# A two-layer transformer kernel: six of the first attention's maxima earlier, constant rows on ACT, one block for keys and heads, earlier first products and a finer last store

## The reference

```python
x = L0_attn_x                                   # 2 x 1024 x 512
xn = _layernorm(x)
x = x + attn0(xn) + ffn0(xn)                    # 16 heads of 32, 4 key heads, full softmax;
                                                # silu(xn@W1.T) * (xn@W3.T), Hadamard, @W2.T
xn = _layernorm(x)
x = x + attn1(xn) + ffn1(xn)                    # 16 heads of 128 (two halves of 64), window 128,
                                                # relu(a1 - lam*a2) renormalised;
                                                # shared expert + top 4 of 32 experts
```

## Time and profile before

| what | value |
|---|---|
| median of 3 runs | 2629.05 us (2627.87 to 2630.51) |
| profiled execution, its own time | 2627.59 us |
| its span | 2625.8 us |
| PE busy | 2483.7 us (95%) |
| DVE, ACT, POOL busy | 1737.8, 1100.6, 1037.9 us |

### The profile page before, as it was taken

One profiled execution on the slowest core, in us unless ns is written; L12 is line 12 of the kernel. 1 busy time (PEld: TensorE's weight loads), 2 busy tenths in 40 slices (PEclk: granted clock), 3 DMA queues, 4 the chain that ended last, 5 costly groups with the idle time before them and its releaser, 6 DMA issues. The chain is left out here.

```text
span 2625.8 us, 35942 instructions
## 1 busy us (share of the span) xinstructions
PE 2483.7 (95%) x12212; PEld 1702.1 (65%) x12212; DVE 1737.8 (66%) x3817; ACT 1100.6 (42%) x2815; POOL 1037.9 (40%) x827
## 2 busy tenths in 40 slices
PE   6899999999799999998989999889999799999998
PEld 3444444444488888886767777667777556657886
DVE  6677676765355555556459999759999633336886
ACT  1246464645233333332327777627777511111111
POOL 2359787876311111110027676525454300002442
PEclk9989999999899999999999999999999999999999
DMA  5722222213200000001212100010000198873111
GB/s 182 243 51 41 57 41 41 41 21 128 105 17 16 16 16 16 16 1 53 74 56 72 35 29 13 18 53 12 17 17 1 39 327 301 295 254 94 49 25 64
DMA packets 170343, 193.64 MB, mean 74 GB/s; under 512 B 85582, under 2 KB 115278, under 8 KB 169792
## 3 DMA queue, kind: packets, MB, share of 16 engines
q1 hardware_dynamic: 158656, 178.90, 22.0%
q0 software_dynamic: 11520, 12.64, 1.5%
HBM read 161.95 MB, written 54.53 MB: 82 GB/s over the span
## 5 line engine op out<-in xcount | busy, mean ns | idle before, releaser
L653 DVE TENSOR_REDUCE neg<-bank 128x1 fp32r<-128x1024 f32 x256 | 300.9, 1214 | 120.7 <-PE bank L556 120.7
L703 ACT ACTIVATE probs<-bank 128x512 f32<-128x512 f32 x512 | 277.8, 595 | 243.9 <-PE bank L566 242.0
L494 POOL TENSOR_TENSOR probs<-probs 128x1024 f32<-128x1024 f32 x128 | 302.8, 2388 | 136.1 <-PE bank L575 135.6
L1643 POOL TENSOR_SCALAR mix<-mix,sm 128x256 f32<-128x256 f32 (+1 forms) x256 | 233.0, 922 | 174.7 <-DVE sm L1541 174.2
L1584 ACT ACTIVATE ms<-ms,sm 128x256 f32<-128x256 f32 (+1 forms) x512 | 247.6, 486 | 111.8 <-DVE sm L1512 110.9
L881 POOL TENSOR_TENSOR up_lo<-up_raw,up_hi 128x1024 fp32r<-128x1024 f32 x16 | 46.2, 2905 | 392.6 <-ACT up_hi L869 392.6
L566 PE MATMUL bank<-q_parts,k_parts 97*128 97x512 f32 x512 | 187.4, 445 | 0.7 <-ACT probs L703 0.7
L1512 DVE CUSTOM_DVE_ANT_0 ms<-bank,misc 128x256 f32<-128x256 f32 (+1 forms) x512 | 184.7, 399 | 2.3
L566 PEld LDWEIGHTS bank<-q_parts,k_parts 97*128 97x128 f32 x512 | 86.9, 189 | 146.2 <-ACT probs L703 84.4
L556 PE MATMUL bank<-k_parts,q_parts 96*128 96x512 f32 x512 | 152.8, 419 | 7.8 <-DVE neg L653 5.9
L1883 POOL TENSOR_TENSOR up_lo<-up_raw,up_hi 128x1024 fp32r<-128x1024 f32 x11 | 26.2, 2381 | 334.5 <-ACT up_hi L1852 334.5
(11 more groups left out here) (227 smaller groups left out, 5841.6 us busy)
## 6 DMA issues: line engine op xcount, KB each, us to landing
ewg<-in_L_ffn_Wg_dram SPq DMA_DIRECT2D x32, 704.0 KB, 6.8
ewu<-in_L_ffn_Wu_dram SPq DMA_DIRECT2D x32, 704.0 KB, 8.0
ewd<-in_L_ffn_Wd_dram SPq DMA_DIRECT2D x32, 512.0 KB, 5.1
q_parts<-qk_dram SPq DMA_DIRECT2D x48, 256.0 KB, 4.4
w_dram<-w_parts SPq DMA_DIRECT2D x16, 512.0 KB, 3.5
up_raw<-in_L_ffn_W_dram SPq DMA_DIRECT2D x16, 512.0 KB, 4.1
ewd<-in_L_ffn_Wd_dram SPq DMA_DIRECT2D x32, 192.0 KB, 5.3
qk_dram<-qk_hi SPq DMA_DIRECT2D x20, 256.0 KB, 2.3
```

The costliest lines, as they stand in the source:

```text
L494: pool.tensor_tensor(probs[:, even, half, :], probs[:, even, half, :], probs[:, odd, half, :], ALU.add).then_inc(S["paired"], 1)
L653: dve.tensor_reduce(neg[:, U % HPT, q:q + 1], bank[:, 2 * (n % 2):2 * (n % 2) + 2, :], AX.XY, ALU.max, negate=True).then_inc(S["max"], 1)
L703: act.activation(probs[:, s % BUFS, j, :], bank[:, 4 + j % 2, :], ACT.Exp, scale=scale).then_inc(S["exps"], 1)
L1643: pool.tensor_scalar(mix[:, p % 2, h, 0:w], mix[:, p % 2, h, 0:w], sm[:, p % 3, 8 + h:9 + h], None, ALU.mult).then_inc(S["probs"], 1)
```

## The change

- The tile `neg` is allocated in the outer scope. In the last chunk of the projection PE makes `early_peaks(f)` behind each of its six products, in banks 4 and 5, and DVE `early_maximum(f)` behind each rotation and, for the last, behind the copy of the values. `heads0` then begins with n = 6 (`EARLY0`).
- POOL no longer fills the rows of ones; ACT writes them, as copies of a broadcast one, in chunk 1 behind the high parts of tiles 3 and 4.
- In both feed-forwards PE waits for a new tile's high part, and for its low part only ahead of the products that read it.
- In the second attention the two blocks of each half become one. PE waits for the rotated keys ahead of the first scores, and in the second half for the reloaded values ahead of the first weighing; SP no longer waits for them.
- In the last step of the second feed-forward PE signals each of the four tiles, DVE waits for each, and SP stores the last chunk tile by tile.

```diff
+EARLY0 = 6
...
+        t["neg"] = sb(ctx, "neg", [P, HPT, CH // P], F32R)
...
+            def early_peaks(n):
+                u, q = n // SUBS, n % SUBS
+                if n == 0:
+                    wait(pe, env["h0"]["q_loaded0"], 48)
+                    wait(pe, env["h0"]["k_loaded0"], 48)
+                wait(pe, env["h0"]["max"], n)
+                for h in range(2):
+                    mm = pe.matmul(bank[:, 4 + h, :], t["qp"][0:3 * HD0, u, q * P:(q + 1) * P],
+                                   t["kp"][0][0:3 * HD0, u % KV0, h * CH:(h + 1) * CH], start=True, stop=True)
+                mm.then_inc(env["h0"]["peaks"], 1)
...
+                    if c == NC - 1:
+                        early_peaks(f)
...
+            def early_maximum(n):
+                wait(dve, env["h0"]["peaks"], n + 1)
+                dve.tensor_reduce(t["neg"][:, n // SUBS, n % SUBS:n % SUBS + 1], bank[:, 4:6, :], AX.XY, ALU.max,
+                                  negate=True).then_inc(env["h0"]["max"], 1)
...
                     turn(c, f)
+                    if not more:
+                        early_maximum(f)
...
                 dve.tensor_copy(vT[:, :], bank[:, NR % 4, :]).then_inc(S["read"], 1)
+            early_maximum(NR)
...
                     act.activation(hi[:, n % KEPT, :], rot[:, f % 2, :], ACT.Copy).then_inc(S["hi"], 1)
+                    if c == 1 and f >= NR - BATCH:
+                        row = t["kp"][f - (NR - BATCH)][3 * HD0:3 * HD0 + 1, :, :].rearrange("p j s -> p (j s)")
+                        act.activation(row, env["ones"][3 * HD0:3 * HD0 + 1, 0:1].to_broadcast([1, KV0 * SEQ]),
+                                       ACT.Copy).then_inc(env["h0"]["const"], 1)
...
-            for b in range(BATCH):
-                pool.memset(t["kp"][b][3 * HD0:3 * HD0 + 1, :, :].bitcast(F32), 1.0).then_inc(env["h0"]["const"], 1)
-                wait(pool, env["h0"]["const"], b + 1)
...
-                for n in range(LEAD * SUBS):
+                for n in range(EARLY0, LEAD * SUBS):
                     peaks(n)
...
-                        wait(pe, S["split"], i * 6 + 3 * a + m + 1)
+                        wait(pe, S["hi"], i * 6 + 3 * a + m + 1)
                     count = 0
                     for l, r in PARTS:
+                        if c == 0 and h == 0 and l:
+                            wait(pe, S["split"], i * 6 + 3 * a + m + 1)
...
                 project_keys_values(env, block, env["h1"], g, t)
-            with nc.Block() as block:
                 attention1_heads(env, block, env["h1"], g, t, r)
...
-        if g:
-            sp.wait_ge(S["kw"], CREDIT + 64)
...
+            if g and p == 0:
+                pe.wait_ge(S["kw"], CREDIT + 64)
...
+        pe.wait_ge(S["qdone"], CREDIT + NC * (g + 1))
         scores(0)
...
-                        pe.wait_ge(S["split"], CREDIT + 2 * h + 1)
+                        pe.wait_ge(S["hi"], CREDIT + 2 * h + 1)
...
+                        if c == 0 and m == 0 and l:
+                            pe.wait_ge(S["split"], CREDIT + 2 * h + 1)
...
-                    mm.then_inc(S["y"], 1)
+                        if n == STEPS - 1 or s == SUBS - 1:
+                            mm.then_inc(S["y"], 1)
...
-                    dve.wait_ge(S["y"], CREDIT + n + 1)
                     for s in range(SUBS):
+                        dve.wait_ge(S["y"], CREDIT + n + 1 + (s if n == STEPS - 1 else 0))
...
+                sp.wait_ge(R["used"], CREDIT + TOPK * NT)
+                for n in range(NT - SUBS, NT):
+                    sp.wait_ge(S["added"], CREDIT + SUBS * STEPS - NT + n + 1)
+                    sp.dma_start(out_v[:, n, :], X[:, n, :]).then_inc(R["out"], 16)
```

More of the change, by code:

```diff
@@ L422, in heads0 @@
         ring = both[:, :].rearrange("p (r h n) -> p r h n", r=RING, n=D)
-        neg = sb(ctx, "neg", [P, HPT, SUBS], F32R)
+        neg = t["neg"]
         den = sb(ctx, "den", [P, CH])
@@ L1758, in _ @@
                 out_v = env["out"].rearrange("b (n p) d -> p (b n) d", p=P)
-                for c in range(NC):
+                for c in range(NC - 1):
                     sp.wait_ge(S["added"], CREDIT + SUBS * (STEPS - NC + c + 1))
@@ L1762, in _ @@
                     sp.dma_start(out_v[:, c * SUBS:(c + 1) * SUBS, :], X[:, c * SUBS:(c + 1) * SUBS, :]).then_inc(R["out"], 16)
-                sp.wait_ge(R["out"], CREDIT + 16 * NC)
+                sp.wait_ge(R["used"], CREDIT + TOPK * NT)
+                for n in range(NT - SUBS, NT):
+                    sp.wait_ge(S["added"], CREDIT + SUBS * STEPS - NT + n + 1)
+                    sp.dma_start(out_v[:, n, :], X[:, n, :]).then_inc(R["out"], 16)
+                sp.wait_ge(R["out"], CREDIT + 16 * (NC - 1 + SUBS))
             @block.tensor
```

## The result

The changed kernel takes **2611.63 us** (median of 4 runs, 2611.08 to 2612.19) against 2628.66 for the kernel before on the same chip: ratio 0.9933, 95% interval 0.9921 to 0.9945. The forecast of 2608 was 3.6 us too low; the range held the time. The profiled execution took 2611.08, its span 2609.3: 16.5 shorter than before, where the sum had 21.2.

A forecast was written before the change was run, and what follows sets the result against it. TensorE, busy 95% of the span, was taken as the bound, so gains come where it stands still or is paced. Terms summed to -21.2 us: 2627.59 to 2606.4, plus 1.5 for the median, forecast 2608, range 2601 to 2615.

The forecast's parts named there:

- 1, fills gone: Start of the projection: without POOL's constant-row fills the last transpose and first product come earlier, 5.7 us gained.
- Step 2: Projection chunk 1: constant rows on ACT delay chunk 2 by 3.5 us, and half clock behind PE's gap costs 1.7.
- Step 3: Last projection chunk: early peaks lengthen five steps by about 0.55 each; chunk and block end about 3.4 us later.
- step 4: First attention's lead-in: DVE waits 4.5 us for shift transfers at the 17th maximum; early peaks' saving is lost, +0.1.
- 5, first feed-forward: Start of the first feed-forward: PE no longer waits for POOL's low part first, 2.4 us gained.
- step 6: Second attention, both halves: with one block DVE's idle before the first query turn goes, everything 5.9 us earlier, 11.9 together.
- 7, second feed-forward: Start of the second feed-forward: PE starts 2.4 us earlier, not waiting for POOL's low part.
- 8, tail: End of the kernel: adds released tile by tile and last store of 256 KB instead of 1 MB, 4.1 us gained.
- The rival by which the lead pays: First attention's lead-in: shift transfers land in time, -4.3 instead of +0.1, so 2603.5 us; chance 0.13.
- The merged block that saves 1 us: Second attention: PE still waits for the rotation before the queries, only about 1 us won twice, 2618; chance 0.06.
- No other phase of the 128 units: Second attention, slower rival: units run in another phase, DVE's query turns wait for PE, up to 2710 us; chance 0.03.
- The table load: Second attention: exponentials' table load might move behind the first mask, 1.28 us once, 2609; chance 0.07. The sum had it hidden.

The follow-up runs named there:

- run 1: The changed kernel without the six early pairs and maxima, so the lead-in again makes all 20: 2611.21 us, ratio 0.9935.
- run 4: The changed kernel with the second batch's keys, two W2 pieces and output weights issued behind the fourth head's shift copies: 2604.07 us, ratio 0.9901.
- run 8: The kernel of run 7 without the six early pairs and maxima: 2600.95 us, ratio 0.9891.
- run 6: The kernel before with only the merged block of the second attention: 2620.59 us against 2629.91, ratio 0.9964.
- run 5: The changed kernel with unread products filling PE's gaps ahead of the second attention's key projections and second query products: 2607.87 us, ratio 0.9918.
- run 9: The changed kernel with both feed-forwards' low-part waits and the tail put back as before: 2618.26 us, ratio 0.9961.
- run 2: The changed kernel with ACT's two constant rows moved to the start, ahead of its first high part: 2606.80 us, ratio 0.9917.
- run 3: The changed kernel with the first head's four shift copies issued ahead of keys, W2 piece and output weights: 2611.75 us, ratio 0.9939.
- run 7: The changed kernel with constant rows at the start, weights behind the fourth head's copies, and unread products in second-attention gaps: 2594.73 us, ratio 0.9863.

## Why the prediction was right, and where it was off

By its own steps, as the lag of the changed kernel behind the kernel before moves from place to place (minus is a gain):

| step | predicted | measured |
|---|---|---|
| 1, fills gone | -5.7 | -5.7 at the first rotation |
| 2, rows on ACT | +3.5 and +1.7 | +3.85 and +2.2 |
| 3 and 4, early peaks and lead-in | +0.1 | +0.6 at the end of the first attention |
| 5, first feed-forward | -2.4 | -2.2 |
| behind 5, in its first products | 0 | -0.4 |
| 6, merged blocks | -11.9 | -12.1, and +4.2 given back to the clock |
| 7, second feed-forward | -2.4 | -2.7 |
| 8, tail | -4.1 | -4.3 |
| sum | -21.2 | -16.5 |

**Right.** That the early start pays for the rows on ACT and no more (steps 1 and 2); that the early peaks give all back to the first head's shift copies, at the 17th maximum (step 4; runs 1, 4 and 8); and the starts of both feed-forwards, the merged block's 6.0 in each half and the tail. The rival by which the lead pays fell because of the queue alone, as its counter-argument said. The merged block that saves 1 us fell too (run 6). No other phase of the 128 units showed: from the first mask to the last product of a half the lag changes by 0.3 at most.

**The mis-sized term is that of step 6.** It asked where PE would stand still and took the products to run at full clock once the block's end was gone ("begins it straight behind the key products and, at full clock, takes half of 5.44"). That held for the first query product. But PE then waits 2.44 for DVE's turn of that product, and the second product ran partly at half clock, 1.48 late; and the second half's key projection, which the change does not touch, lost its full clock behind an idle time of the same 3.40 as before, 2.75 late. Together 4.2, which is nearly all of the 4.7 that the sum was off. Step 2 had priced the clock behind a gap of PE, and step 6 did not. The fills (run 5) show that it is the clock: with them the stretches are at 1.00 and the delays are gone.

**Step 2** was 0.85 short: 0.35 because the rows follow each other on ACT without the overlap that I had taken off, and 0.5 because the slow products cost 2.2, not 1.7. **Step 3** came out smaller: the chunk grew by 2.1 (PE's first pair of the next block goes from 124.60 to 127.11, less the 0.36 of lag), not 3.4. Its five steps grew by 2.7, as forecast (DVE's copy of the values goes from 121.30 to 124.38), but the last maximum runs beside the last transposes. **Step 4** came out larger (DVE waited 6.46, not 4.5), since DVE was ready sooner and could go on at 146.96, not 146.2. For the fourth copy I had taken the median of the four, 6.2 from issue to landing; the fourth itself took 7.0 in the kernel before, and 7.5 now. The two errors nearly cancel, which is luck. So is a part of the forecast's nearness: it added 1.5 us for what the median of the runs lies above the profiled execution, and here that is 0.5, so that a sum 4.7 too low became a forecast 3.6 too low.

**The table load** did move, and stayed hidden. The Trainium skill, "ScalarE activation tables: per-element evaluation and per-set limits", section Table sets in the compiler and the runtime, says that loads are placed per block. In the merged block it stands right behind ACT's last copy of weights, 39 us ahead of the first exponential's row at 1357.15:

```profile
1317.33 1.06 ACT L1371 ACTIVATE w_hi<-w 128x1024 fp32r<-128x1024 f32 x1 [6.04 <-DMA w<-in_L_attn_Wq_dram]
1318.41 1.28 ACT L1610 ACT_TABLE_LOAD   x1
```

## What to carry to other kernels

Work moved to an idle engine is free only where that engine is idle at that time: the same two rows cost 6 us in chunk 1 and nothing 48 us earlier. If a chain is paced by small transfers behind large ones on one queue, shortening its compute gives nothing, and letting one small transfer pass moves the wait to the next; let all of them pass that the chain needs (5.7 us here, and then the early peaks brought 6.2). Price each gap of TensorE twice, by its length and by what the products behind it lose at half clock, also where the change doesn't touch them.

## What the runs showed of the hardware that I had not expected

- **Equal gaps, unequal clocks.** Behind the idle 3.40 of the second half the key rotation came 5.91 us after PE's start in the kernel before, 7.44 and 7.45 in runs 4 and 9, and 8.49 to 8.67 in the changed kernel (both profiles) and runs 1, 2, 3 and 6. Where it was 8.49 and more, the first half's second query product was slow too, and the very first pass behind the idle 3.93 took 0.78 to 0.80; in runs 4 and 9 that pass took 0.49 and 0.55, and the query product was at full clock. So the three places seem to go together in a profile; what sets them was not found. At the start, too, equal instructions differ: the first 24 passes took 10.54 us in eight of the fourteen profiles and 12.19 to 13.12 in the other six. The Trainium skill, "TensorE: Matmul & The Clock Gate", Part 1, says that the moment of a change is not tied to the kernel's start, and this agrees with it.
- **One load's issue held SP for 8 us.** The record of the 1 MB of output weights on SP's queue is 7.89 us long (7.56 and 8.15 in runs 3 and 4), that of the 512 KB ahead of it 0.40. The Trainium skill, "DMA: Bandwidth & Descriptors", section Issuing engines are not separate DMA queues, calls the time to initiate a transfer usually small beside the transfer. Here it is not, 7.9 of the 16.6 us from issue to landing, and everything behind it on that queue is late by it. In five profiles (before, changed, runs 3, 4 and 7) the record ends 0.5 to 0.7 us before the third of the keys' loads, issued ahead of it, lands. That speaks for the loads ahead as the cause, but whether it is they, the size or the layout was not tried.
